# Attention and routed FFN on one core: the q, k, v projection with weights stationary and a rotary step on turned rows

## The chip, the cores and the metric

The kernel runs on one core of a Trainium2 chip. The metric is the device time of one execution in microseconds (us), median of several. The engines are TensorE (PE, its weight loads PEld), VectorE (DVE), ScalarE (ACT), GpSimd (POOL) and SyncE (SP), which here only issues transfers.

## The reference, cut to what matters

One layer in fp32 on 4 batches of 512 tokens of width 256: attention with 32 query heads in 8 groups of 4 (head size 64), each group with one k and one v head, then a routed FFN of 8 experts.

```python
proj = layernorm(x) @ W_qkv                      # 256 -> 2048 (q) + 512 (k) + 512 (v)
q, k, v = split(proj)
q, k = rope(q), rope(k)                          # pairs (d, d+32) of a head; only d < 16 turns
attn = einsum('bqhmd,bkhd->bhmqk', q, k) / 8
attn = where((q_pos >= k_pos) & (q_pos < k_pos + 64), -inf, attn)
w = softmax(concat([attn, sink]))[..., :-1]
x = x + einsum('bhmqk,bkhd->bqhmd', w, v) @ W_out
# then x + MoE(layernorm(x)): gates, top 2, 640 slots per expert, 256 -> 1024 -> 256
```

Rope on a head x of 64: `[x1*cos + x2*sin, -x1*sin + x2*cos]`, x1 and x2 its halves. Its angles are zero for 16 of the 32 pairs.

## The kernel before, in words

The attention is worked in 32 groups g (batch g // 8, kv head g % 8) of 4 query heads and 4 tiles of 128 tokens, so 16 units n (one head, one tile of queries) of 128x512 scores. `all_periods` writes the order of every engine by hand: in period g, step n does step n of group g, step n - 16 of group g + 1 (its preparation) and step n + 16 of group g - 1 (its end), in this order within each step. Every engine runs its own such list and they meet at semaphores only, each engine in strict order.

- TensorE, even steps: the scores of units n and n + 1 in two of three banks (`SCORE`); a pair waits until VectorE is through unit n - 2 (`s_neg_max`). Then what `PV_AT`, `PROJ_AT`, `Y_AT` and `QK_AT` put at the step: PV (16 blocks of 16 matmuls into PV[0] to PV[3]), `project` of one tile of tokens (128 tokens x 384 columns of q, k, v of the group, six matmuls in a split form, high and low parts, with the tokens stationary), the output projection Y, and `turn_qk`, which turns q and k of a tile by three 128x128 transposes. Projection and turn share bank 7.
- VectorE, each step: unit n (mask, scale, row maximum, L820), after each second unit a transpose of two units' probabilities (L831), at step 0 the sink's argument (`sink_arg`, L838), at step 1 the reciprocals (L848 to L855), at steps 10 and 11 `heads_sb` (L864).
- ScalarE, each step: the exponential of unit n (L649), in the call for group g, and behind it, in the call for group g + 1, the projection's copies out of bank 7 (`proj_out`, L633 and L634, at the projection's own step) or of the turned q and k (`qk_out`, L638). `y_sb` (L657) at steps 13 and 15.
- GpSimd: `rotate`, five operations per tile on `qk_sb` (L524 to L532), `split` of the weights two groups ahead (L492, L494), residual additions of 128x512 (L548) at steps 13 and 15; routing's scatters.
- SP, in order: per period `spread_recip` (reciprocals to memory, L383, and back spread, L388), `load_w`, `spread_v` (v to memory and back in four transfers, L366 and L376; the next batch's `xcur` from `x_parts`, L370), in the first eight periods `zero_rows`.

Routing of a finished batch (`pe_route`, `dve_route`, ...) lies in the periods of the next one. Ahead of period 0 stands a prologue (layernorm, transposes of x, group 0's projection, GpSimd's mask and constants; TensorE waits for `s_const` 4 before the gate column, L1143); after period 31 the FFN, which the change does not touch.

Of the kernel before, what the change touches and what calls it, by code (L numbers as in the profile page):

```python
# [20 lines left out]
F32 = mybir.dt.float32  # L21
# [5 lines left out]
P = 128  # L27
# [3 lines left out]
TPB = L // P  # L31
# [23 lines left out]

def moe_layer(nc, x, w_qkv, w_out, sink, gate_w, w1, b1, w2, b2, rope, out):
    ctx = ExitStack()
    with ctx:
# [14 lines left out]
        PV, SCORE, PROJ, QKT = banks[0:4], banks[4:7], banks[7], banks[7]  # L73
# [75 lines left out]
        s_proj_out = sem("s_proj_out")  # L149
        s_rot = sem("s_rot")  # L150
        s_qk_turned = sem("s_qk_turned")
        s_qk_ready = sem("s_qk_ready")
# [60 lines left out]
        rope_sb = sb("rope_sb", [P, TPB, 3, RH], c=actx)  # L213
# [113 lines left out]
        def xT_part(n, part):  # L327
# [3 lines left out]
            if b == 0:  # L331
# [6 lines left out]
        qk_blocks = [buf.rearrange("p s (c a i) -> p s c a i", a=QUADS, i=BLK) for buf in  # L338
                     (qk_st[0][:, :, :], qk_st[1][:, :, :])]
# [5 lines left out]
        def _(sp):  # L345
# [17 lines left out]
            def spread_v(g, j, half):  # L363

                sp.wait_ge(s_proj_out, g * TPB + TPB)
                sp.dma_start(v_rows, v_next[:, :, :].rearrange("p t d -> p (t d)")).then_inc(s_v_out, 16)  # L366
                b, first_of_batch = divmod(g + 1, NKV)
                if first_of_batch == 0 and b < B:
                    sp.wait_ge(s_parts_out, 16 * (B - 1))
                    sp.dma_start(xcur[:, :, :, :].rearrange("p a c q -> p (a c q)").bitcast(F32),  # L370
                                 x_parts[b]).then_inc(s_xcur, 16)
# [6 lines left out]
                sp.wait_ge(s_v_in[j], half * (16 * QUADS) + 16 * QUADS)  # L378

            def spread_recip(g):  # L380

                sp.wait_ge(s_recip, g + 1)
                sp.dma_start(recip_rows, recip_t[:, :]).then_inc(s_recip_out, 16)  # L383
                sp.wait_ge(s_recip_out, g * 16 + 16)
# [6 lines left out]
                sp.wait_ge(s_recip_in, g * 32 + 32)  # L391

            load_w(0, 0)
            sp.dma_start(rope_sb[:, :, :, :], rope).then_inc(s_small_in, 16)
# [12 lines left out]
            load_w(2, 0)  # L407
            for b in range(1, B):
# [4 lines left out]
                if b == 1:  # L413
                    spread_v(0, 0, 0)
# [25 lines left out]
            sp.wait_ge(s_proj, GROUPS * TPB)  # L440
# [3 lines left out]
            spread_recip(GROUPS - 2)  # L444
            spread_recip(GROUPS - 1)
# [26 lines left out]
        def _(pool):  # L472
            steps = [0]

            def own(ins):
# [7 lines left out]
                                    base=0, pattern=[[-1, P]], channel_multiplier=1).then_inc(s_const, 1)  # L483
            own(nc.gpsimd.memset(x2T[:, 0:KC + 1, :], 0.0))
            nc.gpsimd.memset(x2T[:, KC, 0:1].bitcast(U32), int(NOWHERE)).then_inc(s_const, 1)

            def split(g, j, half):

                pool.wait_ge(s_w_in[j], half * 48 + 48)
                if later(g - 1):  # L490
                    pool.wait_ge(s_proj, (g - 1) * TPB)
# [786 lines left out]
```

## Time and profile before

| | us |
|---|---|
| median of 3 runs | 1215.43 |
| lowest and highest run | 1215.41, 1430.16 |
| the profiled execution | 1214.81 |
| its span, first to last instruction | 1212.8 |
| TensorE busy | 1127.7 (93%) |
| VectorE busy | 912.6 (75%) |
| ScalarE busy | 693.8 (57%) |
| GpSimd busy | 593.8 (49%) |

The mean granted clock of TensorE is 0.979 of full speed. Matmuls are pipelined, so their shown durations overlap; the distance between starts says what one costs.

### The profile page before, as it was taken

To read this page: it belongs to the slowest core of one execution; us is meant where nothing else is said; L and a number is where in the kernel's file an instruction comes from. 1 tells how busy PE (TensorE), PEld (TensorE's weight loads), DVE (VectorE), ACT (ScalarE), POOL (GpSimd) and SP (SyncE) were. 2 spreads that over 40 slices of the span, in tenths; PEclk is the share of its full clock that TensorE was granted. 3 is DMA by queue.
4 is the path that set the end of the run, shared out by engine and by line. 5 is a ranking of instruction groups with operands and counts; after the bars stand their busy time and mean duration, and the time that the engine had idled before them with its cause. 6 is when DMAs were issued, how large, how long until landed. Compare 5 with 4: busy or idle time off the path is not lost. (4 is left out here: it accounts for less than half of the span.)

```text
span 1212.8 us, 32000 instructions
## 1 busy us (share of the span) xinstructions
PE 1127.7 (93%) x12859; PEld 776.6 (64%) x12859; DVE 912.6 (75%) x2001; ACT 693.8 (57%) x1773; POOL 593.8 (49%) x884
## 2 busy tenths in 40 slices
PE   2899999999999999999999999999987399999996
PEld 1555655555565555566655555665545399999995
DVE  7588888888898888888888889898885244444442
ACT  1566666666766666675656666666653255454551
POOL 6344454544445654544465444456421555555552
PEclk9899999999999999999999999999998599999998
DMA  8323332431222231222222312122132414444441
GB/s 181 139 76 91 92 92 80 125 91 55 72 59 77 80 94 55 72 72 59 67 74 79 98 54 72 56 69 78 55 111 72 150 16 110 112 111 109 110 110 18
DMA packets 103491, 102.89 MB, mean 85 GB/s; under 512 B 29552, under 2 KB 98352, under 8 KB 102448
## 3 DMA queue, kind: packets, MB, share of 16 engines
q1 hardware_dynamic: 96048, 92.30, 25.5%
q0 software_dynamic: 7296, 8.55, 4.2%
q8 instruction: 102, 1.67, 0.6%
q14 instruction: 45, 0.37, 0.1%
HBM read 76.89 MB, written 24.97 MB: 84 GB/s over the span
## 5 line engine op out<-in xcount | busy, mean ns | idle before, releaser
L649 ACT ACTIVATE probs_ring<-probs_ring,neg_max 128x512 f32<-128x512 f32 x512 | 367.5, 719 | 266.8 <-DVE neg_max L820 263.4
L820 DVE CUSTOM_DVE_ANT_0 probs_ring<-bank,mask,sink_neg 128x512 f32<-128x512 f32 x512 | 366.1, 740 | 108.8 <-PE bank L1082 107.0
L831 DVE STREAM_TRANSPOSE probs_t<-probs_ring 128x1024 f32<-128x1024 f32 x256 | 317.1, 1239 | 0.0
L1082 PE MATMUL bank<-qk_st 64*128 64x512 f32 x1024 | 290.7, 645 | 10.3 <-DVE neg_max L820 7.1
L1101 PE MATMUL bank<-probs_t,v_quads 32*64 32x256 f32 x8192 | 254.7, 382 | 6.5 <-DVE probs_t L831 6.5
L524 POOL TENSOR_TENSOR rot_a<-qk_sb,rope_sb 128x160 f32<-128x160 f32 x128 | 67.9, 530 | 302.5 <-ACT v_next L634 302.0
L1101 PEld LDWEIGHTS bank<-probs_t,v_quads 32*64 32x64 f32 x8192 | 174.6, 132 | 59.8 <-issue 21.7
L1056 PE MATMUL bank<-w_hi,xcur 128*128 128x384 f32 x512 | 169.3, 372 | 3.9 <-ACT v_next L634 2.0
L1056 PEld LDWEIGHTS bank<-w_hi,xcur 128*128 128x128 f32 x512 | 96.8, 193 | 101.5 <-issue 74.5
L548 POOL TENSOR_TENSOR x_sb<-x_sb,y_sb 128x512 f32<-128x512 f32 x64 | 81.8, 1279 | 148.4 <-ACT y_sb L657 148.3
L1082 PEld LDWEIGHTS bank<-qk_st 64*128 64x128 f32 x1024 | 77.5, 185 | 96.2 <-issue 56.8
L1114 PE MATMUL bank<-wo_sb,heads_sb 128*128 128x256 f32 x512 | 121.3, 380 | 0.9 <-DVE heads_sb L864 0.9
L1068 PEld LDWEIGHTS bank<-identity,qk_sb 128*128 128x128 f32 x384 | 40.7, 142 | 98.6 <-issue 95.1
L1114 PEld LDWEIGHTS bank<-wo_sb,heads_sb 128*128 128x128 f32 x512 | 92.4, 190 | 12.8 <-DVE heads_sb L864 2.1
L649 ACT ACTIVATION_READ_ACCUMULATOR probs_ring<-probs_ring,neg_max 128x1 f32 x512 | 97.5, 190 | 0.0
L746 ACT ACTIVATE hidden<-bank,b_sb 128x320 f32<-128x320 f32 x128 | 60.5, 524 | 55.4 <-PE bank L1222 55.4
L1235 PE MATMUL bank<-w_hi,hidden_hi 128*128 128x256 f32 x320 | 90.9, 284 | 0.0
L1235 PE MATMUL bank<-w_hi,hidden_lo 128*128 128x256 f32 x320 | 90.2, 282 | 0.0
L1235 PE MATMUL bank<-w_lo,hidden_hi 128*128 128x256 f32 x320 | 90.2, 282 | 0.0
L638 ACT ACTIVATE qk_st<-bank 128x384 f32<-128x384 f32 x128 | 62.2, 486 | 48.8 <-PE bank L1068 44.6
L1056 PE MATMUL bank<-w_lo,xcur 128*128 128x384 f32 x256 | 88.3, 345 | 0.0
L1222 PE MATMUL bank<-slots_hi,w_hi 128*128 128x320 f32 x256 | 79.8, 312 | 1.4 <-issue 1.4
(129 smaller groups left out, 1682.0 us busy)
## 6 DMA issues: line engine op xcount, KB each, us to landing
v_quads<-v_rows SPq DMA_DIRECT2D x128, 128.0 KB, 2.5
recip_wide<-recip_rows SPq DMA_DIRECT2D x64, 256.0 KB, 4.4
w_raw<-in_L_ffn_w SPq DMA_DIRECT2D x16, 1024.0 KB, 7.0
w_raw<-in_L_attn_W_qkv SPq DMA_DIRECT2D x32, 256.0 KB, 2.7
slot_rows<-x2T SPq DMA_DIRECT2D x8, 662.5 KB, 5.1
slots<-slot_rows SPq DMA_DIRECT2D x8, 662.5 KB, 4.1
w_raw<-in_L_attn_W_qkv SPq DMA_DIRECT2D x64, 64.0 KB, 2.6
v_rows<-v_next SPq DMA_DIRECT2D x32, 128.0 KB, 1.7
```

The lines of the kernel that those rows point to most:

```text
L524: nc.gpsimd.tensor_tensor(a, rot, cos.broadcast_to([P, NH, 2, RH]), ALU.mult).then_inc(s_pool, 1)
L548: nc.gpsimd.tensor_tensor(x_sb[:, t:t + 2, :], x_sb[:, t:t + 2, :], y_sb[half][:, :, :], ALU.add).then_inc(s_residual, 1)
L638: nc.scalar.activation(qk_blocks[j][:, :, :, t, :], QKT[:, 0:3 * P].rearrange("p (s c i) -> p s c i", s=3, i=BLK), ACT.Copy).then_inc(s_qk ...
L649: nc.scalar.activation(probs[n % RING][:, :], probs[n % RING][:, :], ACT.Exp, bias=neg_max[j][:, n:n + 1], scale=-1.0, accum_out=sums[j][: ...
L820: nc.vector.tensor_tensor_reduce(probs[n % RING][:, :], SCORE[SCORE_OF[n // 2][n % 2]][:, :], mask[:, L - P - t * P:2 * L - P - t * P], -S ...
L831: nc.vector.transpose(probs_t[j][:, :, (h // 2) * (2 * P):(h // 2 + 1) * (2 * P)] .rearrange("p b (h q) -> p h b q", h=2)[:, :, :, t * BLK ...
L1056: ins = nc.tensor.matmul(PROJ[:, 0:GW], xcur[:, part, kc, t * P:(t + 1) * P], w[:, kc, :], start=(kc == 0 and m == 0), stop=(kc == KC - 1 ...
L1082: nc.tensor.matmul(SCORE[SCORE_OF[n // 2][hh]][:, :], qk_st[j][half, h // 2, t * P:(t + 1) * P], qk_st[j][half, PAIRS, :], start=True, sto ...
L1101: ins = nc.tensor.matmul(PV[a][p * HD:(p + 1) * HD, 0:2 * P], v_quads[j][rows, c, d * HD:(d + 1) * HD], probs_t[j][rows, blk, p * 2 * P:(p ...
L1114: ins = nc.tensor.matmul(PV[half][:, (a % 2) * D:(a % 2 + 1) * D], heads_sb[:, a, h * P:(h + 1) * P], wo_sb[:, bass.ds((g % NKV) * 2 + h, ...
L1222: ins = nc.tensor.matmul(banks[4 + 2 * (c % 2) + half][:, 0:HALF], w[:, kc, c * P:(c + 1) * P], a[:, at:at + HALF], start=(kc == 0 and m = ...
L1235: ins = nc.tensor.matmul(FFN2[s][:, 0:D], a[:, c, s * P:(s + 1) * P], w[:, c, :], start=(c == 0 and m == 0), stop=(c == HC - 1 and m == 2))
```

## The change

The projection is turned round: the weights are stationary and all 512 tokens of a batch stream through in one matmul. A group has three chunks of 128 weight columns, KV (k and v), Q01 and Q23, and its q and k come out turned (feature by token), so `turn_qk` and `qk_out` go. The rotary step works on turned rows: the partner of a row lies 32 partitions away and is fetched by a transfer (`swap_halves`, 16 rows of 512, two transfers for KV and four for each q chunk); three GpSimd operations of 512 columns follow for each chunk. k is doubled onto the upper 64 partitions by a transfer (`k_twice`). v is turned back by four transposes (`turn_v`) into PV[3] and copied by `v_copy`. PV moves from steps 2, 4, 6, 8 (3, 4, 4, 5 blocks) to 4, 6, 8 (5, 5, 6). SP's order is rewritten, and the final waits of the two spreads are moved ahead of the next write. The rope table grows from 96 KB to 512 KB.

```diff
-        PROJ_AT = {-16: 0, -14: 1, -8: 2, -6: 3}
-        QK_AT = {-12: 0, -10: 1, -4: 2, -2: 3}
-        QK_OUT_AT = {n - 1: t for n, t in QK_AT.items()}
+        PROJ_AT = {-16: KV, -14: Q01, -6: Q23}
+        CHUNK_OUT_AT = {n + 1: c for n, c in PROJ_AT.items()}
+        TURN_V_AT, V_NEXT_AT = -14, -12
+        ROT_AT = {-13: KV, -10: Q01, -2: Q23}
-        for n, blocks in [(18, 3), (20, 4), (22, 4), (24, 5)]:
+        for n, blocks in [(20, 5), (22, 5), (24, 6)]:
-        ROT_AT = {n + 1: t for n, t in PROJ_AT.items()}
+        V_TURNED = [SCORE[0]] + [PV[3]] * (GROUPS - 1)
...
             for g in range(GROUPS - 1):
+                swap_halves(g + 1, KV)
                 if g > 0:
-                    spread_recip(g - 1)
+                    recip_out(g - 1)
+                v_out(g + 1)
+                swap_halves(g + 1, Q01)
+                if g > 0:
+                    recip_spread(g - 1)
+                k_twice(g + 1, (g + 1) % 2)
                 if g + 3 < GROUPS:
                     load_w(g + 3, (g + 3) % 2)
-                spread_v(g + 1, (g + 1) % 2, (g + 1) // 2)
+                v_in(g + 1, (g + 1) % 2)
+                swap_halves(g + 1, Q23)
+                next_batch(g + 1)
...
+                pool.wait_ge(s_chunk_out, q + 1)
+                pool.wait_ge(s_swapped[c], (g + 1) * (32 if c == KV else 64))
...
+                nc.gpsimd.tensor_tensor(straight, straight, rope_sb[rows, 0, :], ALU.mult).then_inc(s_pool, 1)
+                nc.gpsimd.tensor_tensor(swapped, swapped, rope_sb[rows, 1, :], ALU.mult).then_inc(s_pool, 1)
+                pool.wait_ge(s_pool, base + 2)
+                nc.gpsimd.tensor_tensor(qk_st[j][rows, PAIRS if c == KV else c - Q01, :], straight, swapped,
+                                        ALU.add).then_inc(s_rot, 1)
...
-            for t in range(TPB):
-                rotate(0, t)
-                if t == 1:
+            for c in (KV, Q01, Q23):
+                rotate(0, 0, c)
+                if c == Q01:
                     split(1, 1, 0)
...
+            def chunk_out(g, c):
+                q = g * CHUNKS + c
                 act.wait_ge(s_proj, q + 1)
+                if q > 1:
+                    act.wait_ge(s_rot, q - 1)
+                if c == Q23:
+                    act.wait_ge(s_v_turned, g + 1)
+                nc.scalar.activation(chunk_sb[q % 2][:, :].rearrange("p (c a i) -> p a c i", a=QUADS, i=BLK),
+                                     PROJ[:, :].rearrange("p (a c i) -> p a c i", a=QUADS, i=BLK),
+                                     ACT.Copy).then_inc(s_chunk_out, 1)
+
+            def v_copy(g):
+                act.wait_ge(s_v_turned, g + 1)
+                if g > 0:
                     act.wait_ge(s_v_out, g * 16)
+                nc.scalar.activation(v_next[:, :, :], V_TURNED[g][:, 0:TPB * HD].rearrange("p (c d) -> p c d", d=HD),
+                                     ACT.Copy).then_inc(s_v_next, 1)
 
             def act_step(n, g, j):
-                if n in PROJ_AT:
-                    proj_out(g, PROJ_AT[n])
-                if n in QK_OUT_AT:
-                    qk_out(g, j, QK_OUT_AT[n])
+                if n in CHUNK_OUT_AT:
+                    chunk_out(g, CHUNK_OUT_AT[n])
+                if n == V_NEXT_AT:
+                    v_copy(g)
...
                 if later(q):
-                    pe.wait_ge(s_proj_out, q)
-                if later(g * TPB + t // 2 * 2):
-                    pe.wait_ge(s_qk_ready, g * TPB + t // 2 * 2)
+                    pe.wait_ge(s_chunk_out, q)
                 for kc in range(KC):
-                    for m, (part, w) in enumerate([(0, w_hi[j]), (0, w_lo[j]), (1, w_hi[j])]):
-                        ins = nc.tensor.matmul(PROJ[:, 0:GW], xcur[:, part, kc, t * P:(t + 1) * P],
-                                               w[:, kc, :], start=(kc == 0 and m == 0), stop=(kc == KC - 1 and m == 2))
+                    for m, (part, w) in enumerate([(0, w_hi[j]), (1, w_hi[j]), (0, w_lo[j])]):
+                        ins = nc.tensor.matmul(PROJ[:, :], w[:, kc, chunk_cols(c)], xcur[:, part, kc, :],
+                                               start=(kc == 0 and m == 0), stop=(kc == KC - 1 and m == 2))
...
+            def turn_v(g):
+                pe.wait_ge(s_chunk_out, g * CHUNKS + KV + 1)
...
+                for c in range(TPB):
+                    ins = nc.tensor.transpose(V_TURNED[g][:, c * HD:(c + 1) * HD],
+                                              chunk_sb[(g * CHUNKS + KV) % 2][HD:P, c * P:(c + 1) * P],
+                                              identity[HD:P, HD:P])
+                ins.then_inc(s_v_turned, 1)
...
                     if n == 0:
-                        pe.wait_ge(s_qk_ready, (g + 1) * TPB)
+                        pe.wait_ge(s_rot, g * CHUNKS + Q01 + 1)
+                        pe.wait_ge(s_k_twice, g * 16 + 16)
+                    if n == UNITS // 2:
+                        pe.wait_ge(s_rot, g * CHUNKS + Q23 + 1)
...
                         if later(2 * g):
                             pe.wait_ge(s_y_out, 2 * g)
+                        if g + 2 < GROUPS:
+                            pe.wait_ge(s_v_next, g + 2 + 1)
```

In the last hunk g is the group whose PV starts, so in period g + 1 the wait is for the v of group g + 2, which that period prepares.

## Rows read from the trace of the kernel before

**Rows 1.** Timeline of SP: first and 31st of 32 issues at L383, start and duration.

```profile
74.34 0.34 SPq L383 DMA_DIRECT2D recip_rows<-recip_t  x1
...
895.13 0.34 SPq L383 DMA_DIRECT2D recip_rows<-recip_t  x1
```

**Rows 2.** Busy time by window, one period: PE, PEld, DVE, ACT, POOL, clock, DMA.

```profile
155.17:181.95 26.78, 26.65 (x356) 15.88 (x348) 22.96 (x49) 16.88 (x47) 12.86 (x25) 1.00 0.30 87
```

**Rows 3.** Timeline of TensorE, one period: start, duration, operation.

```profile
176.70 1.13 PE L1082 MATMUL bank<-qk_st 64*128 64x512 f32 x4
...
179.02 1.13 PE L1082 MATMUL bank<-qk_st 64*128 64x512 f32 x4
...
182.87 1.13 PE L1082 MATMUL bank<-qk_st 64*128 64x512 f32 x4
...
183.94 0.53 PE L1068 MATMUL bank<-identity,qk_sb 128*128 128x128 f32 x3
...
184.41 1.98 PE L1101 MATMUL bank<-probs_t,v_quads 32*64 32x256 f32 x64
...
189.77 1.13 PE L1082 MATMUL bank<-qk_st 64*128 64x512 f32 x4
...
194.42 1.13 PE L1082 MATMUL bank<-qk_st 64*128 64x512 f32 x4
...
200.19 1.13 PE L1082 MATMUL bank<-qk_st 64*128 64x512 f32 x4
```

**Rows 4.** The same timeline, VectorE, GpSimd and ScalarE after the first score pair.

```profile
177.86 0.75 DVE L820 CUSTOM_DVE_ANT_0 probs_ring<-bank,mask,sink_neg 128x512 f32<-128x512 f32 x1 [0.18 <-PE bank L1082]
...
178.19 1.29 POOL L548 TENSOR_TENSOR x_sb<-x_sb,y_sb 128x512 f32<-128x512 f32 x1 [0.77 <-ACT y_sb L657]
...
178.54 0.96 DVE L838 TENSOR_TENSOR sink_arg<-neg_max,sink_all 128x16 f32<-128x16 f32 x1
...
178.66 0.72 ACT L649 ACTIVATE probs_ring<-probs_ring,neg_max 128x512 f32<-128x512 f32 x1 [0.55 <-DVE neg_max L820]
...
179.43 0.74 DVE L820 CUSTOM_DVE_ANT_0 probs_ring<-bank,mask,sink_neg 128x512 f32<-128x512 f32 x1
...
180.10 1.23 DVE L831 STREAM_TRANSPOSE probs_t<-probs_ring 128x1024 f32<-128x1024 f32 x1
```

**Rows 5.** Chain of waits, FFN: start, length, matmuls of 320 and 256 columns.

```profile
993.12 14.09 PE bank L1222 x96
...
1038.37 14.24 PE bank L1235 x120
```

**Rows 6.** View by line, L838: duration in ns, least, median, most.

```profile
L838 DVE TENSOR_TENSOR sink_arg<-neg_max,sink_all x32: 128/956/1394, 71.7 to 915.3; 128x16 f32<-128x16 f32 x32
```

**Rows 7.** Groups by line and shape, ScalarE's copies out of PSUM: busy us, mean ns.

```profile
L638 ACT ACTIVATE qk_st<-bank 128x384 f32<-128x384 f32 x110 | 53.4, 485 | 42.2 <-PE bank L1068 38.9
...
L657 ACT ACTIVATE y_sb<-bank 128x512 f32<-128x512 f32 x54 | 32.1, 594 | 1.1
```

**Rows 8.** DMA issues: count, KB each, median us from issue to landing.

```profile
v_quads<-v_rows SPq DMA_DIRECT2D x128, 128.0 KB, 2.5
...
xcur<-x_parts SPq DMA_DIRECT2D x3, 1024.0 KB, 5.4
```

**Rows 9.** Timelines of the prologue, TensorE and GpSimd: start, duration.

```profile
30.77 1.97 PE L1037 MATMUL bank<-identity,xn 128*128 128x128 f32 x8 [6.50 <-DVE xn L807]
...
43.43 0.20 POOL L574 MEMSET ones<- 128x128 f32 x1
...
44.57 0.38 POOL L584 CAST before_r<-before 128x128 fp32r<-128x128 f32 x1
...
46.63 1.02 PE L1143 MATMUL bank<-gate_sb,ones 128*128 128x8 f32 x4 [1.34 <-DVE probs_t L812]
```

**Rows 10.** Busy time by window near the end of attention; clock after POOL.

```profile
918.00:920.00 2.00, 2.00 (x52) 1.50 (x46) 0.00 (x0) 0.00 (x0) 0.00 (x0) 0.50 0.06 8
```

**Rows 11.** Timeline of TensorE there.

```profile
916.68 8.85 PE L1101 MATMUL bank<-probs_t,v_quads 32*64 32x256 f32 x256 [2.46 <-DVE probs_t L831]
```

More of the change, by code:

```diff
@@ L53 @@
 BLOCKS = L // BLK
+KV, Q01, Q23 = 0, 1, 2
+CHUNKS = 3
 def moe_layer(nc, x, w_qkv, w_out, sink, gate_w, w1, b1, w2, b2, rope, out):
@@ L148, in moe_layer @@
         s_proj = sem("s_proj")
-        s_proj_out = sem("s_proj_out")
+        s_chunk_out = sem("s_chunk_out")
+        s_swapped = [sem(f"s_swapped{i}") for i in range(CHUNKS)]
         s_rot = sem("s_rot")
-        s_qk_turned = sem("s_qk_turned")
-        s_qk_ready = sem("s_qk_ready")
+        s_k_twice = sem("s_k_twice")
+        s_v_turned = sem("s_v_turned")
+        s_v_next = sem("s_v_next")
         s_scores = sem("s_scores")
@@ L336, in moe_layer, with chunk_cols @@
         NORM_BANKS = banks[0:4]
-        qk_blocks = [buf.rearrange("p s (c a i) -> p s c a i", a=QUADS, i=BLK) for buf in
-                     (qk_st[0][:, :, :], qk_st[1][:, :, :])]
+        V_TURNED = [SCORE[0]] + [PV[3]] * (GROUPS - 1)
+        def chunk_cols(c):
+            return slice(QM * HD, GW) if c == KV else slice((c - Q01) * P, (c - Q01) * P + P)
         block = ctx.enter_context(nc.Block())
@@ L407, in _ @@
             load_w(2, 0)
+            sp.wait_ge(s_const, 2)
+            swap_halves(0, KV)
+            v_out(0)
+            swap_halves(0, Q01)
+            k_twice(0, 0)
+            v_in(0, 0)
             for b in range(1, B):
@@ new lines, in _, with rotate @@
+            ROT_STEPS = 2
+            def rotate(g, j, c):
+                q = g * CHUNKS + c
+                rows = slice(0, HD) if c == KV else slice(0, P)
+                pool.wait_ge(s_chunk_out, q + 1)
+                pool.wait_ge(s_swapped[c], (g + 1) * (32 if c == KV else 64))
+                if c == KV and g > 1:
+                    pool.wait_ge(s_scores, (g - 1) * UNITS)
+                straight, swapped = chunk_sb[q % 2][rows, :], swap_sb[q % 2][rows, :]
+                base = before_group + q * ROT_STEPS
+                nc.gpsimd.tensor_tensor(straight, straight, rope_sb[rows, 0, :], ALU.mult).then_inc(s_pool, 1)
[3 more added lines that the diff above has]
+                                        ALU.add).then_inc(s_rot, 1)
@@ L665, in _ @@
                 norm_hi(n)
-            proj_out(0, 0)
-            proj_out(0, 1)
+            chunk_out(0, KV)
             root(1)
@@ L670, in _ @@
                 norm_hi(n)
-            qk_out(0, 0, 0)
-            qk_out(0, 0, 1)
-            proj_out(0, 2)
-            proj_out(0, 3)
+            v_copy(0)
+            chunk_out(0, Q01)
             for n in range(2 * TPB, 3 * TPB):
                 norm_hi(n)
-            qk_out(0, 0, 2)
-            qk_out(0, 0, 3)
+            chunk_out(0, Q23)
             for n in range(3 * TPB, 4 * TPB):
@@ L1252, in rope_tables @@
     theta = np.arange(L, dtype=np.float32)[:, None] * freq[None, :]
-    tables = np.stack([np.cos(theta), np.sin(theta), -np.sin(theta)], axis=1).astype(np.float32)
-    return np.ascontiguousarray(tables.reshape(TPB, P, 3, RH).transpose(1, 0, 2, 3))
+    tables = np.zeros((P, 2, L), np.float32)
+    tables[:, 0, :] = 1.0
+    for p in range(P):
+        first, r = p % HD < HD // 2, p % (HD // 2)
+        if r < RH:
+            tables[p, 0] = np.cos(theta[:, r])
+            tables[p, 1] = np.sin(theta[:, r]) if first else -np.sin(theta[:, r])
+    blocks = tables.reshape(P, 2, TPB, QUADS, BLK).transpose(0, 1, 3, 2, 4)
+    return np.ascontiguousarray(blocks.reshape(P, 2, L))
 _INS = ["L0_attn_x", "L0_attn_W_qkv", "L0_attn_W_out", "L0_attn_s", "L0_ffn_gating_w",
```

138 lines of the change are left out of this document (57 added, 81 removed).

## The prediction, made before the change was run

> **What bounds the kernel now.** The page's busy line, in the table above, has TensorE at 93% of the span and VectorE at 75%; which of them sets the time has to be read from one stage. The timeline shows a regular period per group of heads: the reciprocals' transfer to memory, issued once a period, goes out at 74.34 us for the first time and at 895.13 us for the 31st, so 30 periods take 820.8 us, 27.36 us each [rows 1]. A period without routing work, 155.17 to 181.95, takes 26.78 us, with TensorE busy for 26.65 and VectorE for 22.96 at a clock of 1.00 [rows 2]. The rest, before 74 us and after 895 us, has little projection in it.
>
> Next comes the order of TensorE's work in one period. Call S0, S2, ... S14 the starts of its score pairs (step n = 0, 2, ... 14). They stand at 176.70, 179.02, 182.87, 189.77 (S8), 194.42 (S10), 200.19 (S14), and the next S0 at 203.48 [rows 2, 3]. The pieces: a score pair 1.06 us (182.87 to 183.94); a tile's projection 2.32 - 1.06 = 1.26; a turn of q and k 0.47 (183.94 to 184.41); S4 to S8 is two steps of 3.45, each pair + turn + 4 PV blocks, so a block is 0.48. S10 to S14 takes 5.77 where the pieces make less: there VectorE (two units, a transpose, heads, again) is the bound. Elsewhere TensorE is.
>
> The third view is the loop through the other engines. VectorE starts a unit 1.16 us after its S (176.70 to 177.86) and ScalarE its exponential 0.80 us later (178.66); that takes 0.72 [rows 4]. Nothing on TensorE waits for an exponential of the same step now; this is where the change bites.
>
> **The change, step by step.** *Projection.* 24 matmuls of 384 columns become 18 of 512. Two runs of the same split form give the rate: 96 matmuls of 320 columns in 14.09 us, 146.8 ns each, and 120 of 256 in 14.24, 118.7 ns [rows 5]. That is 0.44 ns per column, so 231 ns at 512 (175 at 384). A chunk keeps the head and tail of today's: 1.26 + 5 x (0.231 - 0.175) = 1.54. Three chunks are 4.6 us, four tiles 5.0. The Trainium skill, TensorE: Matmul & The Clock Gate, section on the back-to-back issue gap, gives about 131 ns sustained at 512 columns; the rows, with 147 ns at only 320, disagree. By it (an estimate) a chunk would be 0.5 us shorter and the end some 15 us earlier, since only one chunk of three lies bare.
>
> *Turns.* Four turns (1.9 us) go; turn_v, four small transposes, comes. No row has its shape; I put it between one turn of three transposes (0.47) and two (0.94). I take 0.55.
>
> *PV.* 16 blocks stay 7.7 us, but they leave step 2: 5, 5 and 6 blocks at steps 4, 6, 8. So TensorE alone saves 0.4 + 1.35 = 1.7 us a period, 50 us in all, if nothing else waits.
>
> *First new wait, step 2.* project(Q01) waits for chunk_out(KV), which ScalarE issues at step 1 **behind exp(1)**; today it waits for a copy behind exp(0). exp(1) needs unit 1, which starts at S0 + 2.73 (179.43), because sink_arg before it takes 0.96 [rows 4]. The copy has 512 columns, as y_sb's 594 ns [rows 7]. Release: 2.73 + 0.80 + 0.72 + 0.59 + 0.1 = S0 + 4.94, and 5.13 because VectorE is some 0.2 late into S0: from unit 12, which releases S14 0.8 us later, it has four units (0.67 apart, 179.43 to 180.10) and two transposes (1.2) to do, 5.0 us, so unit 0 comes at S14 + 4.2, while S0 + 1.16 is S14 + 4.0. TensorE is there at S0 + 2.60 + 1.06 = 3.66: it idles for 1.5. S4 comes at 5.13 + 1.54 + 0.55 = S0 + 7.2, where it was 6.17: **+1.05**.
>
> *Second new wait, step 4.* turn_v borrows PV[3], so the first PV block waits for s_v_next, the count of v_copy(g+1). ScalarE issues v_copy at the same step 4, **behind exp(4) of the running group**, and exp(4) needs the scores that TensorE has only just made. The loop: S4 + 1.16 (unit 4 starts) + 0.80 + 0.72 (exp) + 0.38 (copy of 256 columns, on the line from 384 at 485 ns and 512 at 594 [rows 7]) + 0.1 = S4 + 3.15. Scores end at S4 + 1.06, so TensorE idles for 2.1 us, and behind it are queued all of PV and the next scores, so VectorE starves too. S4 to S6: 3.15 + 2.40 = 5.55, was 3.45: **+2.1**. It is a circle through three engines, not a resource: no earlier work shortens it.
>
> *Remaining steps.* S6 to S8: 1.06 + 2.40, unchanged. S8 to S10: 1.06 + 2.88 = 3.94, was 4.65: **-0.7**. S10 to S14: bound by VectorE, 5.77 again (a chunk for a tile, no turn). S14 to S0: no turn, 2.83, was 3.29: **-0.46**. Sum: 1.05 + 2.1 - 0.7 - 0.46 = **+2.0 us a period**, and 30 periods (g = 1 to 30) have both waits: +60. The routing extra (27.36 against 26.78) I carry over.
>
> *GpSimd.* Nine tensor operations of 512 columns at 1.29 us (the residual addition at 178.19 [rows 4]) replace 20 shorter ones: 11.5 us, with split and residual 17 of some 29 us. It fits. Q23's chunk is copied about 4.8 us after S10, swapped 3.6 us later and rotated in 3 x 1.28, behind the first residual addition: done about 4 us into the next period, and needed at its step 8. Q01's, behind KV's rotation and the split, is done near S0 + 18 and needed at the next S0. So this edit costs nothing by itself; were that cover gone, each late us at either place would be one of the period. It does touch VectorE: sink_arg takes 128 ns at best, 956 in the median, 1394 at most [rows 6]; the one of 0.96 starts at 178.54, inside the addition on GpSimd (178.19 to 179.48), and ends with it [rows 4]. The Trainium skill says why, GPSIMD Engine Reference, Key points: GpSimd shares its SBUF interfaces with VectorE operations of two SBUF inputs; the trace agrees. By that rule the busier GpSimd holds sink_arg and denom more often. Bounds of the first wait: sink_arg never held, -0.83 a period; held for 1394 ns and denom too, +0.6.
>
> *SP.* A swap is four issues (two for KV) of some 0.4 us each (0.34 for the smallest [rows 1]); the v_quads transfers land 2.5 us after their issue with four times a swap's data [rows 8]. So a swap is through 3.6 to 4.1 us after its chunk, beside the work above. recip_spread now stands behind v_out and swap Q01 (about S0 + 12.5, landed before 18; heads need it at 21): covered. v_in waits for PV as before. The next batch's xcur goes out behind swap Q23, near S0 + 26.5, and lands 5.4 later [rows 8], 2 us after project(KV) wants it; the first wait absorbs most: +0.6, three times, +2.
>
> *Prologue.* TensorE takes up the gate column at 46.63, after GpSimd's constants (43.43 to 44.95) [rows 9]. Now GpSimd must first rotate Q01. Its projection comes behind the turns of the second four tiles (30.77 to 32.5 [rows 9]) and turn_v, at the lower clock: 6 x 512 columns / 1.2 GHz = 2.6 us and a tail, the copy 0.6: out near 36.9, swapped at 40.5, rotated at 44.4. Then come the split (768 columns: 1.9 for its subtraction at the rate of the addition above, and a cast, 2.6 in all; to 47.0) and Q23 (to 50.9); constants end at 52.4: **+5.8**, bounds 2 (swaps overlap better) and 9. The epilogue has no projection: 0.
>
> **Sum.** 60 + 2 + 6 = 68 on a span of 1212.8: 1281; with the 2.0 us that the profiled execution (1214.81) has around its span 1283. The median of the runs is 0.6 above that execution; I say 1282.
>
> **Rivals.**
> 1. *The waits don't bind* (ScalarE's copies are there when TensorE comes). Then S0 to S4 is 2.6 + 3.15, S4 to S6 3.46: 25.2 a period, -1.6 x 30 = -47, +8 outside: 1176, faster. For it: ScalarE is only half busy. Against it: order, not load, holds the copies. It decides if v_copy and chunk_out(KV) run before the exponentials of their steps. Both waits together must shrink from 3.6 to under 1.3 us (3.6 less 68 / 30) for the sign to turn. 0.07.
> 2. *The waits bind, but short*: sink_arg free (-0.83), copies and turn_v at low ends (-0.6): +0.57 a period, 17, with 4 outside: 1236, within 2%. For it: sink_arg's best row; against it: its median. 0.10.
> 3. *The clock falls in the gaps.* After a gap of 2.46 us near the end the granted clock was 0.50 (1.2 GHz) in 918 to 920, and 256 PV matmuls took 8.85 us where 64 take 1.91 (7.65 for 256) [rows 3, 10, 11]: 1.2 us lost. Gaps of 1.5 and 2.1 us within 7 us are near that, though shorter. In every period: +36, 1318; in some: in between. 0.12.
> 4. *GpSimd or SP turns late* (a rotation reaches step 8, or v_out holds the swaps), another 1 us a period: 1312. For it: twice the length per operation; against it: at least 10 us of slack at both places. 0.05.
>
> **How the numbers follow.** My forecast has 0.66. Its own range: the first wait's bounds (-0.83 to +0.6) x 30 = -25 to +18, prologue -4 to +3: 1253 to 1303. Rival 2 takes the low end to 1238, a part of rival 3 the high end to 1312; left out are rival 1, and the ends of 3 and 4. Two per cent, about what can be told from no change here, is 24 us: faster 0.07, same 0.10, slower 0.83.
>
> **What would show it.** In the trace of after: a period of 28.8 us instead of 26.78 without routing; idle time of TensorE before the first PV block of each period, about 2.1 us, released by ScalarE's v_next; about 1.5 us before the second chunk, released by chunk_sb; VectorE waiting longer for scores; 18 matmuls at 0.23 us; GpSimd operations of 1.28 us; first scores near 53 us; clock still 1.00 in the periods. The forecast is wrong if v_next is there when the scores end, or if a third wait (rotations, xcur) shows in TensorE's list.

## The result, and the profile of the kernel after

The changed kernel takes 1341.06 us (median of 4 runs, 1339.28 to 1343.46) where the kernel before takes 1215.68: a ratio of 1.103 (95% interval 1.101 to 1.106). The forecast was 1282, with 1312 as the upper end: the sign was right, the size 59 us short, and the range missed. One of the four runs of the kernel before took 1430.16 us, a slow one, and is left out of the comparison.

The page of the kernel after, its first lines and the granted clock in 40 slices (tenths of full speed):

```profile
span 1338.6 us, 30760 instructions
...
PE 1125.8 (84%) x12411; PEld 754.2 (56%) x12411; DVE 931.8 (70%) x2001; ACT 643.0 (48%) x1517; POOL 710.0 (53%) x534
...
PEclk9789999899999999989989899899998769999998
```

TensorE's busy share fell from 93% to 84%, and VectorE's from 75% to 70%; only GpSimd's rose, from 49% to 53%. No engine is fuller than TensorE was: the time is idle time. It is placed by the mark of [rows 1], SP's issue of the reciprocals, first and 31st in the timeline of SP:

```profile
84.83 0.58 SPq L415 DMA_DIRECT2D recip_rows<-recip_t  x1
...
1017.55 0.34 SPq L415 DMA_DIRECT2D recip_rows<-recip_t  x1
```

The 30 periods take 932.7 us, 31.09 each (before 820.8, 27.36): +111.9. What lies ahead of the first mark is 10.5 us longer, what follows the 31st 3.4. Busy time by window: three whole periods without routing work, then three stretches of 2 us inside the period that begins at 171.99 (columns as in [rows 2]: TensorE, its weight loads, VectorE, ScalarE, GpSimd, granted clock, DMA share, GB/s).

```profile
112.92:143.27 30.35, 26.62 (x327) 15.07 (x326) 23.63 (x49) 15.27 (x39) 16.39 (x13) 0.94 0.34 91
143.27:171.99 28.72, 25.02 (x327) 14.47 (x327) 23.65 (x49) 15.27 (x39) 16.41 (x13) 1.00 0.38 97
233.72:267.62 33.90, 27.59 (x322) 15.69 (x320) 23.42 (x48) 15.38 (x39) 16.35 (x13) 0.87 0.43 113
174.00:176.00 2.00, 0.00 (x0) 0.00 (x0) 2.00 (x6) 1.53 (x6) 1.92 (x3) 1.00 0.00 0
176.00:178.00 2.00, 1.79 (x40) 1.67 (x48) 0.78 (x1) 0.77 (x3) 1.99 (x2) 0.64 0.27 82
178.00:180.00 2.00, 2.00 (x48) 1.52 (x32) 0.00 (x0) 0.00 (x0) 1.81 (x1) 0.51 0.22 49
```

At clock 1.00 this period is 28.72 us, and the forecast said 28.8. The same instructions take 30.35 at clock 0.94. The third, 33.90 at 0.87, also holds a wait of 3.75 us for the next batch's xcur (below), so not all of its excess is the clock's. TensorE's timeline has a period at full clock, S0 to S0 of the next, and below it the first PV blocks one period on:

```profile
137.12 1.13 PE L1127 MATMUL bank<-qk_st 64*128 64x512 f32 x4
...
139.76 1.13 PE L1127 MATMUL bank<-qk_st 64*128 64x512 f32 x4
142.05 0.73 PE L1097 MATMUL bank<-xcur,w_hi 128*128 128x512 f32 x2 [1.16 <-ACT chunk_sb L678]
...
147.50 2.42 PE L1148 MATMUL bank<-probs_t,v_quads 32*64 32x256 f32 x80 [2.48 <-ACT v_next L686]
149.85 1.13 PE L1127 MATMUL bank<-qk_st 64*128 64x512 f32 x4
...
165.84 1.13 PE L1127 MATMUL bank<-qk_st 64*128 64x512 f32 x4
...
176.21 4.11 PE L1148 MATMUL bank<-probs_t,v_quads 32*64 32x256 f32 x80 [2.49 <-ACT v_next L686]
```

Both new waits stand there, 1.16 and 2.48 us, with the releasers that the forecast named. But of two groups of five PV blocks behind the same gap of 2.5 us, one takes 2.42 us and the other 4.11: there the clock went from 1.00 to 0.64 and 0.51, that is to 1.2 GHz. All 30 periods in which the copy is waited for have such a row: 11 show 2.42, and 19 show 3.29 to 4.58, 30.0 us above 2.42 in sum. The list of waits of the whole span (engine, tile and line, releaser: us in total, times, longest) has the two, VectorE's idle time behind them (209.5 us, before 107.0), and two smaller ones:

```profile
DVE probs_ring L863 <- PE bank L1127: 209.5, 105, 5.9
...
PE bank L1148 <- ACT v_next L686: 70.2, 30, 3.3
...
PE bank L1097 <- ACT chunk_sb L678: 31.0, 27, 1.3
...
PE bank L1186 <- POOL before_r L629: 12.5, 1, 12.5
...
PE bank L1097 <- issue: 8.5, 3, 3.8
```

The last is xcur. In TensorE's timeline the first matmuls of a new batch:

```profile
262.81 1.19 PE L1097 MATMUL bank<-xcur,w_hi 128*128 128x512 f32 x2 [3.75 <-issue]
```

Last, the timelines of VectorE and, in the second fence, of ScalarE up to the second wait:

```profile
141.75 0.84 DVE L891 TENSOR_TENSOR denom<-sums,sink_exp 128x16 f32<-128x16 f32 x1
...
144.35 1.24 DVE L874 STREAM_TRANSPOSE probs_t<-probs_ring 128x1024 f32<-128x1024 f32 x1
145.52 0.71 DVE L863 CUSTOM_DVE_ANT_0 probs_ring<-bank,mask,sink_neg 128x512 f32<-128x512 f32 x1
...
151.01 0.75 DVE L863 CUSTOM_DVE_ANT_0 probs_ring<-bank,mask,sink_neg 128x512 f32<-128x512 f32 x1 [2.94 <-PE bank L1127]
```

```profile
146.27 0.72 ACT L696 ACTIVATE probs_ring<-probs_ring,neg_max 128x512 f32<-128x512 f32 x1 [0.47 <-DVE neg_max L863]
...
147.00 0.36 ACT L686 ACTIVATE v_next<-bank 128x256 f32<-128x256 f32 x1
```

The scores of S4 (143.82) were ready for unit 4 at some 145.0, by the 1.16 us of the forecast; VectorE came to it at 145.52, with no pause since S0, and exp(4) (146.27) and v_copy (147.00) follow from there. VectorE's own queue lies close beneath both waits, and in it denom, 0.84 us where the kernel before has 0.13 (128 ns in the median).

### The profile page after: what moved, and what is told of

Same layout as the page of the kernel before. It is cut to its first block and busy times, and to the rows that moved or that the text cites. A ratio compares the mean times of both kernels' runs of the same rounds, so it can differ in the third digit from the quotient of the medians.

```text
span 1338.6 us, 30760 instructions
## 1 busy us (share of the span) xinstructions
PE 1125.8 (84%) x12411; PEld 754.2 (56%) x12411; DVE 931.8 (70%) x2001; ACT 643.0 (48%) x1517; POOL 710.0 (53%) x534
## 5 line engine op out<-in xcount | busy, mean ns | idle before, releaser
L863 DVE CUSTOM_DVE_ANT_0 probs_ring<-bank,mask,sink_neg 128x512 f32<-128x512 f32 x512 | 366.1, 740 | 211.3 <-PE bank L1127 209.5
L1148 PE MATMUL bank<-probs_t,v_quads 32*64 32x256 f32 x8192 | 286.0, 417 | 75.0 <-ACT v_next L686 70.2
L1127 PE MATMUL bank<-qk_st 64*128 64x512 f32 x1024 | 304.7, 661 | 21.6 <-DVE neg_max L863 20.3
L1148 PEld LDWEIGHTS bank<-probs_t,v_quads 32*64 32x64 f32 x8192 | 206.7, 144 | 182.7 <-issue 151.3
L573 POOL TENSOR_TENSOR chunk_sb<-chunk_sb,rope_sb 128x512 f32<-128x512 f32 (+1 forms) x96 | 122.5, 1276 | 140.1 <-DMA swap_sb<-chunk_sb 71.4
L1097 PE MATMUL bank<-xcur,w_hi 128*128 128x512 f32 x384 | 136.5, 438 | 40.5 <-ACT chunk_sb L678 31.0
L1127 PEld LDWEIGHTS bank<-qk_st 64*128 64x128 f32 x1024 | 84.8, 192 | 113.0 <-issue 73.8
L1097 PEld LDWEIGHTS bank<-xcur,w_hi 128*128 128x128 f32 x384 | 68.0, 197 | 126.5 <-issue 61.8
L576 POOL TENSOR_TENSOR qk_st<-chunk_sb,swap_sb 128x512 f32<-128x512 f32 (+1 forms) x96 | 122.1, 1272 | 7.5
L1161 PEld LDWEIGHTS bank<-wo_sb,heads_sb 128*128 128x128 f32 x512 | 92.1, 189 | 58.4 <-issue 44.7
L574 POOL TENSOR_TENSOR swap_sb<-swap_sb,rope_sb 128x512 f32<-128x512 f32 (+1 forms) x96 | 122.8, 1279 | 0.0
L645 POOL TENSOR_TENSOR w_lo<-w_raw,w_hi 128x2048 fp32r<-128x2048 f32 x8 | 36.8, 4597 | 86.7 <-ACT w_hi L767 75.7
```

Of the source, the lines that this page charges most:

```text
L573: nc.gpsimd.tensor_tensor(straight, straight, rope_sb[rows, 0, :], ALU.mult).then_inc(s_pool, 1)
L574: nc.gpsimd.tensor_tensor(swapped, swapped, rope_sb[rows, 1, :], ALU.mult).then_inc(s_pool, 1)
L576: nc.gpsimd.tensor_tensor(qk_st[j][rows, PAIRS if c == KV else c - Q01, :], straight, swapped, ALU.add).then_inc(s_rot, 1)
L863: nc.vector.tensor_tensor_reduce(probs[n % RING][:, :], SCORE[SCORE_OF[n // 2][n % 2]][:, :], mask[:, L - P - t * P:2 * L - P - t * P], -S ...
L1097: ins = nc.tensor.matmul(PROJ[:, :], w[:, kc, chunk_cols(c)], xcur[:, part, kc, :], start=(kc == 0 and m == 0), stop=(kc == KC - 1 and m = ...
L1127: nc.tensor.matmul(SCORE[SCORE_OF[n // 2][hh]][:, :], qk_st[j][half, h // 2, t * P:(t + 1) * P], qk_st[j][half, PAIRS, :], start=True, sto ...
```

## The experiments

Theory A: two waits made by ScalarE's order cost about 2 us a period, and the falls of the clock behind the second cost the rest. Theory B: the second wait only shows what something else sets. Later, once the waits were gone, theory H: VectorE, held up by GpSimd's long operations, is the bound.

### Copy v two steps earlier on ScalarE (e_vcopy)

```diff
-        TURN_V_AT, V_NEXT_AT = -14, -12
+        TURN_V_AT, V_NEXT_AT = -14, -14
```

v_copy then stands behind exp(2), not exp(4).

> One constant of the changed kernel: v_copy goes from ScalarE's step 4 (behind exp(4)) to step 2 (behind exp(2)). Theory A (order plus clock): the changed kernel's periods are 28.7 us where the granted clock stays at 1.00, as forecast, and 31.1 in the mean because the clock falls in the gaps at steps 2 and 4. With the gap before PV gone (2.5 us) and only that at the second chunk left (1.2), a period takes 26.5 to 27.2 with the clock near 1.00: 1215 to 1235. Rival B (GpSimd, held VectorE operations and transfers cost the surplus over 28.7, the waits only their forecast price): 1341 less 30 x 2.4 is 1269. Rival C (another wait stands right behind v_next): no change, 1341.

Measured: 1224.26 us, ratio to the kernel before 1.009 (1.005 to 1.012). One constant gives back 117 of the 125 us. The PV wait is gone from TensorE's list, the clock of the execution is 0.968 (after: 0.94), and the mean period 27.29 us. A holds, its period just above the 26.5 to 27.2 that it allowed; B's 1269 and C's 1341 are far off. The wait at the second chunk is still there (31.8 us in 27 times) and costs little: the 30 periods together are 2 us shorter than before's.

### Copy K and V out before exp(1) (e_kvout)

```diff
-        CHUNK_OUT_AT = {n + 1: c for n, c in PROJ_AT.items()}
+        CHUNK_OUT_AT = {-16: KV, -13: Q01, -5: Q23}
```

> chunk_out(KV) goes from ScalarE's step 1 (behind exp(1)) to step 0 (behind exp(0)); v_copy stays at step 4. Theory A: the gap at the second chunk (1.2 us) closes, but in the changed kernel VectorE runs without a pause from step 10 to unit 4, and v_copy hangs on unit 4, so PV starts no earlier: the gap before PV grows by what the other loses, to 3.7 us, the period stays at 28.7 with the clock at 1.00, and the one long gap lets the clock fall as often or more: 1330 to 1350. Rival D (both waits add up, as the prediction had it): 1341 less 30 x 1.2 is 1305, and less with the clock.

Measured: 1355.74 us, 1.113 (1.108 to 1.119), some 15 us more than the changed kernel and 6 above A's range. TensorE's timeline of this kernel, S0, S4 and the first PV blocks:

```profile
135.62 1.13 PE L1127 MATMUL bank<-qk_st 64*128 64x512 f32 x4
...
142.34 1.13 PE L1127 MATMUL bank<-qk_st 64*128 64x512 f32 x4 [0.98 <-DVE neg_max L863]
...
146.02 4.10 PE L1148 MATMUL bank<-probs_t,v_quads 32*64 32x256 f32 x80 [2.55 <-ACT v_next L686]
```

The chunk's wait is gone, and in its place S4 waits 0.98 us for VectorE; the second gap is as long as before (A had it grow to 3.7). PV starts 10.40 us after S0 (135.62 to 146.02), where it is 10.38 in the changed kernel (137.12 to 147.50). The first wait therefore gates nothing by itself: it sits on top of VectorE's queue. D is out. But now 28 of 30 first PV groups are above 2.42 us (3.46 to 4.58). Two near gaps on TensorE, 0.98 and 2.55 us with one score pair between, find the clock low more often than 1.16 and 2.48 with a chunk, a turn and a pair between.

### Both orders mended (e_both)

The two edits above together.

> Both moves together. Theory A: no gap over 0.5 us is left, the clock stays at 1.00, a period without routing takes 25.2 to 25.7 (TensorE's 24.8 and short waits for VectorE) and 26.2 in the mean: 1341 less 30 x 4.9 is 1194, range 1180 to 1210, so under the kernel before (1215). Rival B (surplus from GpSimd and transfers): 25.5 plus the surplus of 1.8 in the mean, 27.9: 1245.

Measured: 1219.08 us, 1.004 (1.002 to 1.005). Both theories miss: A by 25 (its range ended at 1210), B by 26. TensorE's timeline, then the rows of sink_arg and denom by their tiles (ns, least, median, most):

```profile
133.23 1.13 PE L1127 MATMUL bank<-qk_st 64*128 64x512 f32 x4 [0.95 <-DVE neg_max L863]
134.44 2.42 PE L1148 MATMUL bank<-probs_t,v_quads 32*64 32x256 f32 x80
```

```profile
L881 DVE TENSOR_TENSOR sink_arg<-neg_max,sink_all x32: 130/1032/1058, 77.0 to 919.9; 128x16 f32<-128x16 f32 x32
...
L891 DVE TENSOR_TENSOR denom<-sums,sink_exp x32: 125/534/862, 79.2 to 921.1; 128x16 f32<-128x16 f32 x32
```

With the waits gone VectorE is the bound from S14 over S0 to S4, and two operations that take 0.13 us alone take 1.03 and up to 0.86 on that path. That is theory H, tried below.

### Work for TensorE in the gap (e_fill)

```diff
-                        if g + 2 < GROUPS:
-                            pe.wait_ge(s_v_next, g + 2 + 1)
...
+                        if g + 2 < GROUPS:
+                            for f in range(4):
+                                half = slice(f % 2 * HD, (f % 2 + 1) * HD)
+                                nc.tensor.matmul(PV[f % 2][:, :], qk_st[1 - j][half, 0, 0:P],
+                                                 qk_st[1 - j][half, PAIRS, :], start=True, stop=True)
                             pe.wait_ge(s_v_next, g + 2 + 1)
```

The wait for v_next now stands behind the four matmuls and behind three waits of routing work that it used to precede; no wait goes. PV's later start overwrites what the matmuls leave. (In the rows each of these fp32 matmuls counts twice, so four are x8; so do PV's, whose five blocks, x80, are 40 instructions, and the "16 matmuls" of a block further up are 8.)

> The changed kernel with its waits as they are; ahead of TensorE's wait for v_next it does four matmuls of 512 columns on q and k of the running group into PV[0] and PV[1], whose results PV overwrites (about 2.1 us of work in a gap of 2.5). Theory A: the order and every wait stay, but the gap is filled, so the clock stays at 1.00 and the surplus over 28.7 goes: 1341 less 30 x 1.7 is 1290, range 1275 to 1305, though TensorE has more work. Rival B: the surplus has nothing to do with the clock, no gain: 1341 or a little more.

Measured: 1293.00 us, 1.065 (1.062 to 1.069): 48 us less than the changed kernel, with more work on TensorE. Its timeline:

```profile
140.07 1.95 PE L1144 MATMUL bank<-qk_st 64*128 64x512 f32 x8
142.70 2.42 PE L1152 MATMUL bank<-probs_t,v_quads 32*64 32x256 f32 x80 [0.67 <-ACT v_next L686]
```

None of the 17 first PV groups whose row names the wait takes more than 2.42 us, nor do the 13 others up to the 30th period, and the granted clock between 100 and 900 us is 0.99 (changed kernel: 0.95). The 30 periods are 44.7 us shorter, 1.5 each. That is the price of the falls in the changed kernel; the time before PV is held by the same loop as ever.

### The rest of the way: constants first, xcur earlier (e_all, e_xcur)

e_all is e_both with GpSimd's constants (ones, before_r and the rest) ahead of group 0's rotations; e_xcur adds:

```diff
-                swap_halves(g + 1, Q23)
                 next_batch(g + 1)
+                swap_halves(g + 1, Q23)
```

> Both moved copies, and GpSimd's constants (0.2 to 0.3 us each, 1.4 together) ahead of group 0's rotations instead of behind them. In the changed kernel TensorE stood for 12.5 us before the gate column and began its scores at 54.4 us, 6.8 later than the kernel before. Theory A (prologue bound by s_const): now the scores wait for the rotation of Q01 only (done near 45.3), so they start near 47 and the time falls by 5 to 7 against both moves alone (1219): 1213. Rival: the prologue is bound by something else (k_twice, w_lo of group 1 near 48): 1217 to 1219.

> The same, and SP issues the next batch's xcur ahead of the swap of Q23 instead of behind it. In the changed kernel the transfer left 2.5 us after the swap's first issue and TensorE stood for 3.8 us before the first chunk of a new batch; the period in which that lies is 3.7 us longer than its neighbours with both moves, in the first batch, and 2.2 in the others. Theory A: the wait shortens by 2.5 each, three times: 5 to 8 us less than with the constants alone: 1207. Rival: the swap is late then and TensorE waits for Q23's rotation at step 8: no gain.

Measured: 1211.28 us, 0.998 (0.997 to 0.999), and 1204.83, 0.992 (0.990 to 0.995). The constants were worth 7.8 us (6.9 by the two ratios to the kernel before), and xcur 6.5, over three batches; both theories A hold. In e_all the first scores start at 44.26, where e_both has 52.25, and what they wait for is the rotation (2.2 us, POOL qk_st).

### Shorter operations on GpSimd (e_small, e_short, e_res)

e_small is e_xcur with each rotation in six operations of 256 columns in place of three of 512.

```diff
-                nc.gpsimd.tensor_tensor(straight, straight, rope_sb[rows, 0, :], ALU.mult).then_inc(s_pool, 1)
-                nc.gpsimd.tensor_tensor(swapped, swapped, rope_sb[rows, 1, :], ALU.mult).then_inc(s_pool, 1)
+                for f in range(2):
+                    s = slice(f * W, (f + 1) * W)
+                    nc.gpsimd.tensor_tensor(straight[:, s], straight[:, s], rope_sb[rows, 0, s], ALU.mult).then_inc(s_pool, 1)
+                    nc.gpsimd.tensor_tensor(swapped[:, s], swapped[:, s], rope_sb[rows, 1, s], ALU.mult).then_inc(s_pool, 1)
```

> The same, and GpSimd's rotation runs in operations of 256 columns, six per chunk (0.73 us each by the line through 1.28 at 512 and 0.53 at 160), so its total grows by some 0.55 us a chunk but each operation ends sooner. Theory H (VectorE's sink_arg and denom are held until the running GpSimd operation ends, 1.03 and 0.53 to 0.82 us in the median against 0.13 at best, and VectorE is the bound of the loop now): the holds shrink by half, 0.5 to 0.8 us a period, 15 to 20 us less: 1190. Rival: longer total time of GpSimd, holds as before or more of them: 1207 or more.

Measured: 1187.79 us, 0.978 (0.976 to 0.981), 17 us less for the same arithmetic in more instructions: theory H holds, and with e_res below this is the fastest kernel here. Rows by tile of e_small:

```profile
L887 DVE TENSOR_TENSOR sink_arg<-neg_max,sink_all x32: 134/636/1212, 68.9 to 887.9; 128x16 f32<-128x16 f32 x32
...
L897 DVE TENSOR_TENSOR denom<-sums,sink_exp x32: 126/439/772, 70.8 to 889.1; 128x16 f32<-128x16 f32 x32
```

In e_xcur the medians were 1031 and 846 ns: 0.8 us a period gone from the two, and the mean period went from 26.90 to 26.44, 13.7 us over the 30; the rest lies ahead of them and behind.

e_short is e_both with the rotations on 128 of their 512 columns, so the rest of q and k is not computed (it stays zero); it takes load from GpSimd.

> Both moved copies (no change to the constants and xcur); GpSimd's rotation works on 128 of the 512 columns and leaves out the other three quarters, so part of q and k is not computed; a fill of qk_st with zeros goes ahead in the prologue. All waits, transfers, copies and TensorE's work stay. Theory H: sink_arg and denom run free (0.13 to 0.4 us), VectorE's loop from step 10 to unit 4 shortens by up to 1.5 us and TensorE's work (25.2) becomes the bound: periods of 25.3 where 26.3 stand, less in the periods with routing too: 1219 less 30 to 40 is 1184. Rival (GpSimd's length costs nothing): 1219, or 1215 for the shorter prologue.

Measured: 1199.36 us, 0.988 (0.986 to 0.989): 20 us less than e_both, so the rival is out, but 15 us above what was expected. Timelines of VectorE and, below, of GpSimd show why:

```profile
175.02 1.17 DVE L883 TENSOR_TENSOR sink_arg<-neg_max,sink_all 128x16 f32<-128x16 f32 x1
...
177.95 0.13 DVE L893 TENSOR_TENSOR denom<-sums,sink_exp 128x16 f32<-128x16 f32 x1
```

```profile
174.87 1.28 POOL L595 TENSOR_TENSOR x_sb<-x_sb,y_sb 128x512 f32<-128x512 f32 x1
```

denom is free (0.13), and sink_arg, begun 0.15 us after the residual addition, ends with it (176.19 against 176.15). What holds is the operation that happens to run, not GpSimd's load. That called for e_res: e_small with that addition in two halves.

```diff
-                    nc.gpsimd.tensor_tensor(x_sb[:, t:t + 2, :], x_sb[:, t:t + 2, :], y_sb[half][:, :, :],
-                                            ALU.add).then_inc(s_residual, 1)
+                    nc.gpsimd.tensor_tensor(x_sb[:, t:t + 1, :], x_sb[:, t:t + 1, :], y_sb[half][:, 0:1, :],
+                                            ALU.add)
+                    nc.gpsimd.tensor_tensor(x_sb[:, t + 1:t + 2, :], x_sb[:, t + 1:t + 2, :], y_sb[half][:, 1:2, :],
+                                            ALU.add).then_inc(s_residual, 1)
```

> The version with rotations of 256 columns, and the residual additions on GpSimd in halves too (two of 256 columns for one of 512). Theory H: in the run with short rotations of 128 columns the addition of 1.28 us still held sink_arg for 1.17, so with halves sink_arg falls to 0.7 or less; VectorE is hardly the bound any more (periods of 25.45 against TensorE's 25.2), so 0 to 0.25 us a period: 1180 to 1188. Rival: more instructions on GpSimd cost more than they give: 1190.

Measured: 1188.27 us, 0.979 (0.977 to 0.981), no different from e_small. sink_arg did not fall as expected: its worst case went from 1212 down to 790 ns, but its median rose from 636 to 769: halves make a long hold impossible and a hold of one half likelier. The periods together stayed the same (792.97 us for 30 against 793.22).

### The same wait, put into the kernel before (b_pv, b_wait)

b_pv is the kernel before with PV at steps 4, 6 and 8 alone; b_wait adds a wait of the first PV block for exp(4) of the running group, the condition under which the changed kernel's PV starts.

```diff
-        for n, blocks in [(18, 3), (20, 4), (22, 4), (24, 5)]:
+        for n, blocks in [(20, 5), (22, 5), (24, 6)]:
```

```diff
+                        if g + 1 < GROUPS:
+                            pe.wait_ge(s_probs, (g + 1) * UNITS + 5)
```

> The kernel BEFORE the change with one table altered: PV at steps 4, 6, 8 with 5, 5, 6 blocks, as the change has it, not 3, 4, 4, 5 at steps 2, 4, 6, 8. It is the base for the next run. Theory A: step 2 then has less TensorE work than VectorE's pace needs and steps 4 to 8 more; by the durations S10 comes 1.2 us later, so a period of 28.0 instead of 26.8: 1250, range 1230 to 1255. Rival: VectorE takes up the shift, no change: 1215.

> The same, and the first PV block of a period waits for the exponential of unit 4 of the running group, on data that it does not need: the change's second wait alone, on the old projection, without rotary transfers, longer GpSimd operations or v_copy. Theory A (a circle through three engines in each period, and a gap that lets the clock fall): PV starts near S0 + 9.3 where it could at 7, so 2 to 3 us a period above the run with PV moved, and 1 to 2 more for the clock: 1330 to 1390, granted clock 0.95 or below. Rival B (the new projection's transfers and GpSimd make the loss): within 15 us of the run with PV moved, clock as there.

Measured: b_pv 1263.09 us, 1.040 (1.038 to 1.042), 8 above its range; b_wait 1379.84, 1.133 (1.128 to 1.138), inside A's. In b_pv TensorE waits 47.5 us in all for neg_max (before: 7.1), 1.22 us ahead of S4: with PV gone from step 2, VectorE is behind at S4. That is the same wait that e_kvout and e_both lay bare. b_wait is 117 us above it. One first PV group in TensorE's timeline of b_wait, and the stretch 100 to 900 us (columns as above):

```profile
168.80 4.58 PE L1103 MATMUL bank<-probs_t,v_quads 32*64 32x256 f32 x80 [1.56 <-ACT probs_ring L649]
```

```profile
100.00:900.00 800.00, 718.46 (x8486) 433.04 (x8490) 582.33 (x1291) 430.55 (x1183) 330.88 (x607) 0.91 0.23 65
```

The gap for the exponential adds 51.4 us over 31 times, less than half of the 117; the clock went from 1.00 (b_pv, same stretch) to 0.91, and 30 of the 31 first PV groups take 3.66 to 4.58 us, 53.9 above 2.42 in sum. One wait for one exponential brings the loss to a kernel that has, besides the moved PV blocks of its base, nothing else of the change.

## Why the prediction was right, and where it was wrong

Starts within the period at full clock, against the forecast's steps (us):

| step | forecast | after |
|---|---|---|
| S0 to S4 (wait, second chunk, turn_v) | 7.2 | 6.70 |
| S4 to S6 (v_next) | 5.55 | 6.03 |
| S6 to S8 | 3.46 | 3.40 |
| S8 to S10 | 3.94 | 3.84 |
| S10 to S14 | 5.77 | 5.77 |
| S14 to S0 | 2.83 | 2.98 |
| period | 28.75 | 28.72 |

**The two waits, right.** 1.16 and 2.48 us against 1.5 and 2.1. S4 came half a microsecond earlier than forecast (the second chunk started 0.2 earlier, and it and turn_v take 1.77 us, not 2.09), VectorE did not, and the second gap took up the difference: S4 to S6 is 0.5 over. 512 columns took 0.23 us, as the line through [rows 5] gave. (The figure of the Trainium skill, TensorE: Matmul & The Clock Gate, Back-to-back issue gap, about 131 ns, is not seen here.) The loop account, +1.94 x 30 = 58 us, is right to 2 us for periods like the one in the table, and e_vcopy confirms which edit carries it.

**The clock: the step that failed.** The sum had no term for it: it put the clock at 1.00 in the periods, and the profile shows it at 0.95 between 100 and 900 us (1.00 before), which is worth some 45 us. Rival 3 had the mechanism and its place, with a chance of 0.12 and a price of 1.2 us in every period. The price was read from one row, 8.85 us for 256 PV matmuls against 7.65 [rows 10, 11]: one fall once, in a stretch with nothing behind it. In the loop the first PV group alone loses up to 2.2 us (4.58 - 2.42; 1.0 in the mean of 30), and e_fill prices the falls at 1.5 us a period over all periods, 45 us. [Rows 10] was the evidence, the gaps of forecast and of row had the same length within 0.4 us, and "though shorter" was no reason for 0.12. Even in full rival 3 was short: 1318. Forecast plus e_fill's 45 is 1327, and the rest is in the terms below.

**GpSimd, "this edit costs nothing by itself": wrong.** Its queues were on time, as said. But sink_arg (median 1032 ns, was 956 [rows 6]) and denom (818 ns, was 128) are held in VectorE's queue from S14 to S4. In the changed kernel that shows as the half microsecond by which unit 4 is late, and it is the half that S4 to S6 has above its forecast; no run took it out of that kernel, but one of its own periods does. There denom fell beside a scatter of GpSimd's (slot_rows, 485.63 to 486.63) and not beside an addition. Its row in VectorE's timeline, then the windows of that period and of the one in the table, S0 to S0:

```profile
485.92 0.13 DVE L891 TENSOR_TENSOR denom<-sums,sink_exp 128x16 f32<-128x16 f32 x1
```

```profile
481.28:509.35 28.07, 25.03 (x328) 14.48 (x327) 23.00 (x49) 15.28 (x40) 17.46 (x15) 1.00 0.32 83
137.12:165.84 28.72, 25.00 (x327) 14.46 (x326) 23.64 (x49) 15.26 (x40) 16.42 (x14) 1.00 0.38 96
```

With denom free the gap before PV is 1.82 us, not 2.48, S4 to S6 takes 5.53, as forecast, and the period is 0.65 shorter at the same clock. With the waits gone, e_small shows 17 us for shorter holds. The forecast named them only as a bound of the first wait, at +0.6.

**The first wait's meaning, half wrong.** I took ScalarE's order as what held S4. e_kvout takes it away and gains nothing, and b_pv finds S4 held by VectorE in the kernel before once PV has moved, at 48 us for that move alone: the 1.7 us a period that the forecast gave to TensorE "if nothing else waits" met VectorE at once. (No run put PV back to step 2 in the changed kernel.) The term came out near its number (S4 at 6.70) because two causes of about the same length lie there, one of which I had seen. Rival 1, in which neither wait binds, would have had no 25.2 us period: e_both, which is that case, has 27.21 in the mean, and its 1219 is 43 above rival 1's 1176.

**xcur: mis-sized.** A third wait in TensorE's list, one of the forecast's own signs of being wrong. I had +2 for three batches; it stands 3.75 us late (8.5 us in three) and not covered by the first wait, since project(KV) comes ahead of it. e_xcur gave back 6.5. SP took 2.46 us to issue the four parts of the swap before it, where I had 1.6.

**Prologue: +10.5 ahead of the first mark, forecast +5.8.** The first scores stand at 54.42 (forecast 53.4), and 47.58 before: +6.8, one more than forecast. From there to the next S0 is 24.5 us where it was 21.9, in which TensorE waits 5.1 us for VectorE's neg_max (before 3.0) and neither new wait shows; and the first mark itself is 1.0 late behind its S0, because SP issues KV's swap (83.63 to 84.79) ahead of it. I had priced only the periods between the marks. Tail: +3.4, forecast 0. It lies between the 31st mark and the 32nd and last: 25.78 us there, 22.48 before, while what follows is equal. b_pv has 26.30 there, so the PV move alone is enough for it.

**What stays open.** Why the same gap of 2.5 us leaves the clock at 1.00 in one period and not in the next. Length bears on it (behind gaps of 1.82 and 1.93 us 6 of 13 first PV groups were slow, behind 2.48 to 3.29 us 13 of 17), but no run here separates it. The sum 58 + 45 (e_fill) + 6.5 (e_xcur) = 109.5 of 111.9 closes, but the holds in the periods with routing were not priced apart, and 58 takes every period as held.

## What to carry to other kernels

When a copy releases a bank for another engine, look at what it stands behind in its own engine's order: put behind an exponential that needs the waiting engine's same step, it closes a circle that costs the whole round trip each period, and two steps earlier in the list it costs almost nothing (here one constant gave back 117 us, clock and all). Price a gap on TensorE twice, once by its length and once by what the granted clock does behind it: a row that shows the fall once, at a like gap, is to be taken as the likely case for every period. And an idle time that sits on another engine's queue can be removed and gain nothing, so look beneath it before counting on it.

## What the runs showed of the hardware that was not expected

- Five PV blocks (x80) take 2.42 us at the full clock and up to 4.58 at 1.2 GHz. After gaps of 1.8 to 3.3 us, 19 of 30 were slow; after gaps of 0.65 to 1.42 us behind filler work, none of 17 was. In b_wait gaps of 1.37 to 2.24 us, most of them 1.56, with 0.5 to 1.9 us of idle one score pair earlier, were followed by slow groups in 30 of 31 periods.
- Idle time can be dearer than work: 120 filler matmuls (four a period) made the changed kernel 48 us faster.
- A VectorE operation on 128x16 elements with two inputs in SBUF ends with the GpSimd operation that runs when it starts (175.02 + 1.17 against 174.87 + 1.28), so that its length, 0.13 to 1.2 us, is set by the length of the other engine's instruction. The Trainium skill, GPSIMD Engine Reference, Key points, names the shared interfaces; the trace agrees. A scatter that GpSimd issues does not hold it (0.13 us at 485.92).
- Cutting a GpSimd operation in two helps or not by where the held operation falls in it: with halves of the rotations the time fell by 17 us, with halves of the residual addition by none.
